# A fused scan and expert kernel on one core: the tile loop written out, its table read in place, and the silu turn and state sums moved between the two up-projections

## The reference, cut to what matters

```python
xn = layernorm(x)                                   # x: 2 x 2048 tokens of 256
# branch 1: a selective scan over tokens sorted by cluster
sort_idx = argsort(argmax(l2norm(xn) @ l2norm(means).T))
u = xn[sort_idx];  dts, Bm, Cm = split(u @ x_proj.T);  Cm += prompt[cluster]
delta = softplus(dts @ dt_w.T + dt_b);  A = -exp(A_logs)          # 16 states per channel
h = exp(delta * A) * h + delta * u * Bm             # one step per token, in order
y = sum_over_states(h * Cm) + Ds * u;  out1 = y[inverse of sort_idx]
# branch 2: two of eight experts for each token
out2[t] = sum over the 2 best e of p[t, e] * ((silu(xn @ w1[e]) * (xn @ w3[e])) @ w2[e])[t]
return x + out1 + out2
```

## Time and profile before

| | us |
|---|---|
| median of 3 runs | 819.19 (817.54 to 819.56) |
| the profiled execution | 817.38 |
| its span, first to last instruction | 815.3 |
| DVE busy in the span | 682.9 (84%) |
| PE busy | 663.9 (81%), matmuls |
| POOL busy | 597.3 (73%) |
| ACT busy | 431.0 (53%) |

### The profile page before, as it was taken

The page is one execution under the profiler, slowest core; times in us unless marked ns, Lnnn a source line. Parts: engine busy times, 40 slices in busy tenths (PEclk is TensorE's granted clock), DMA queues, the critical chain, the costliest instruction groups (busy, mean ns, idle before and its releaser), DMA issues. The chain is left out here.

```text
span 815.3 us, 15751 instructions
## 1 busy us (share of the span) xinstructions
PE 663.9 (81%) x4538; PEld 422.7 (52%) x4539; DVE 682.9 (84%) x882; ACT 431.0 (53%) x926; POOL 597.3 (73%) x372
## 2 busy tenths in 40 slices
PE   3734889788998798989998898999889798989870
PEld 2523745245655465556655565565556555655550
DVE  5769777579999999999999999999999999997110
ACT  1324656465655556656655575566557554653320
POOL 3728800038788898988989898888989898889532
PEclk9866955599999989999999998999999998999995
DMA  7972659979944754674575466547645654662322
GB/s 228 371 259 91 180 206 297 321 221 241 210 102 103 144 118 87 146 150 94 115 163 111 89 149 138 105 90 164 139 90 125 134 127 90 142 142 35 49 27 26
DMA packets 76845, 118.63 MB, mean 146 GB/s; under 512 B 22456, under 2 KB 56848, under 8 KB 74512
## 3 DMA queue, kind: packets, MB, share of 16 engines
q1 hardware_dynamic: 54656, 90.95, 41.2%
q0 software_dynamic: 19824, 27.16, 19.4%
q10 hardware_dynamic: 2336, 0.15, 0.2%
HBM read 82.87 MB, written 35.27 MB: 145 GB/s over the span
## 5 line engine op out<-in xcount | busy, mean ns | idle before, releaser
L534 POOL TENSOR_TENSOR ring<-ring,bc 128x1024 f32<-128x1024 f32 (+2 forms) x128 | 308.0, 2424 | 38.9 <-DVE state L1047 38.0
L1044 DVE TENSOR_TENSOR_SCAN ring<-ring,state,pb 128x512 f32<-128x512 f32 x256 | 313.8, 1267 | 4.6
L654 ACT ACTIVATE ring<-late,aneg 128x512 f32<-128x512 f32 x256 | 164.2, 721 | 12.0 <-DMA late<-dd_d 9.1
L1035 DVE TENSOR_TENSOR pb<-fb,bc 128x1024 f32<-128x1024 f32 x128 | 157.3, 1229 | 3.0
L1284 PE MATMUL py<-w2x,pool 128*128 x568 | 141.6, 395 | 0.5 <-ACT pool L726 0.3
L1267 PE MATMUL fa<-w,pool 128*128 x284 | 137.7, 608 | 3.9 <-issue 2.8
L506 POOL DMA_INDIRECT out_dram<-pool,meta x71 | 112.9, 1590 | 29.8 <-issue 15.7
L1267 PE MATMUL fb<-w,pool 128*128 x284 | 134.3, 596 | 0.0
L486 POOL DMA_INDIRECT pool<-xn_d,meta x71 | 71.3, 1004 | 81.3 <-DVE ids L1001 33.5
L1284 PEld LDWEIGHTS py<-w2x,pool 128*128 128x128 f32 x568 | 107.7, 200 | 13.6 <-issue 1.0
L1267 PEld LDWEIGHTS fb<-w,pool 128*128 128x128 f32 x284 | 54.5, 192 | 68.9 <-issue 68.9
(11 more groups left out here) (213 smaller groups left out, 752.8 us busy)
## 6 DMA issues: line engine op xcount, KB each, us to landing
late<-dd_d SPq DMA_DIRECT2D x256, 128.0 KB
bc<-bc_d SPq DMA_DIRECT2D x72, 256.0 KB
w<-in_L_ffn_w_dram SPq DMA_DIRECT2D x16, 512.0 KB, 8.6
ring<-in_L_attn_x_dram SPq DMA_DIRECT2D x8, 512.0 KB, 4.3
out_dram<-ring SPq DMA_DIRECT2D x8, 512.0 KB, 7.7
xn_d<-w2x SPq DMA_DIRECT2D x8, 512.0 KB, 8.6
dd_d<-pool SPq DMA_DIRECT2D x8, 512.0 KB
dd_d<-ring SPq DMA_DIRECT2D x8, 512.0 KB, 5.1
```

The costliest lines, as they stand in the source:

```text
L534: ins = po.tensor_tensor(r, r, c_rows, ALU.mult)
L654: ins = ac.activation(ring[:, g % RING, n, :], dd[:, g % 2, 0, :], ACT.Exp, scale=aneg[:, NH * g + n:NH * g + n + 1])
L1035: ve.tensor_tensor(pb[:, :].rearrange("p (n c) -> p n c", n=2), pd[:, :].rearrange("p (o c) -> p o c", o=1).to_broadcast([P, 2, CH]), b_ro ...
L1044: ve.tensor_tensor_scan(r, r, pb[:, CH * m:CH * m + CH], state[:, NH * g + n:NH * g + n + 1], ALU.mult, ALU.add).then_inc(S["scan_done"], 1)
```

## The change

- **Written out**: the loops are gone on all engines. 64 units and 71 tiles are straight code.
- **The table read in place**: POOL and ACT read `tab` themselves; `meta` and its 71 small transfers are gone. `ids` is read in place too, `ya` has two buffers, and `hand_over` with its two copies a chunk is gone. Gathered rows have 6 buffers (`XR`) and not 4, the scaled results 3 (`YE`) and not 2.
- **Another lag**: unit `u` now goes with tile `j = u - 1` and not `u + 1`. DVE starts unit 0 before any silu, and after unit 63 eight tiles are left (before: six). ACT starts with `put_du(0)`, `exps(0)`, and waits there for less.
- **PE's order in a tile**: `turn_h(j - 1)`, `turn_y` and `fold_states` now stand between the `w1` and the `w3` matmuls of tile `j`. In unit numbers, tile `v + 1` has `fold_states(v)` ahead of its `w3` matmuls.
- **Scan adds**: in steps 3 and 6 of a chunk (before 3 and 7). The last chunk's four go out together after the add of tile 65, not one by one between expert adds.
- **The last unit**: DVE multiplies its last two states by the C rows, POOL the first two. In the tiles after the scan, `turn_x` uses bank `pb`.

```diff
+UNITS = NCH * G
+REST = UNITS + 1
+SCAN_UNITS = {3: (0, 1), 6: (2, 3)}
+XR, XT, YE = 6, 4, 3
@@ sync @@
-            turn(0)
-            with sp.Fori(1, NCH) as c:
-                turn(c)
+            for u in range(UNITS):
+                c, g = u // G, u % G
+                if u >= 2:
+                    load_dd(u)
+                if c == 0 and g + EARLY < E:
+                    load_up(g + EARLY, w3, w3_in)
+                    load_down(g + EARLY)
...
@@ gpsimd @@
+            for u in range(UNITS):
+                c, g = u // G, u % G
+                j = u - 2
+                if j >= 0:
+                    gather(j + XR)
+                scans = SCAN_UNITS.get(g, ()) if c else ()
+                split = 1 if scans else NH // 2
+                po.wait_ge(S["h_ready"], u + 1)
+                done = multiply(u, slice(0, split))
+                for n in scans:
+                    add_scan(c - 1, n, landed_scan(c - 1, scans[0]) - 16)
+                if u < UNITS - 1:
+                    done = multiply(u, slice(split, NH))
+                elif split < NH // 2:
+                    done = multiply(u, slice(split, NH // 2))
+                done.then_inc(S["hc_done"], 1)
+                if j >= 0:
+                    add_expert(j)
+            for j in range(UNITS - 2, FT):
+                if j + XR < FT:
+                    gather(j + XR)
+                add_expert(j)
+                if j == LAST_SCANS:
+                    for n in range(TPC):
+                        add_scan(NCH - 1, n, landed_expert(j))
@@ scalar @@
+            def exps(u):
+                ac.wait_ge(dd_in[u % 2], 64 * (u // 2 + 1))
+                if u == 0:
+                    ac.wait_ge(S["pr_du"], KC * NCH)
+                elif u == 1:
+                    ac.wait_ge(S["bc_put1"], 32 * NCH // 2)
+                    ac.wait_ge(S["dd_put10"], 16 * NCH // 2)
+                elif u == 2:
+                    ac.wait_ge(S["dd_put11"], 16 * NCH // 2)
+                if u >= RING:
+                    ac.wait_ge(S["sum_done"], u - RING + 1)
...
+            put_du(0)
+            exps(0)
+            evac_xt(0)
+            exps(1)
+            for u in range(1, FT + 1):
+                j = u - 1
+                tanh(j)
+                if u < UNITS:
+                    put_du(u)
+                if j:
                     evac_ht(j - 1)
+                if 3 <= u < UNITS + 3:
+                    take_y(u - 3)
+                if 2 <= u < UNITS + 2:
+                    take_sum(u - 2)
                 if j + 1 < FT:
+                    evac_xt(j + 1)
+                if u + 1 < UNITS:
+                    exps(u + 1)
+                if j:
+                    evac_y(j - 1)
@@ vector @@
-            silu(0, 0)
...
+            for u in range(UNITS):
+                if u:
+                    silu(u - 1)
+                half_unit(u, 0)
+                half_unit(u, 1)
+                keep_states(u)
...
+            for j in range(UNITS - 1, FT):
+                silu(j)
@@ tensor @@
+            def sums_and_turns(u):
+
+                pe.wait_ge(S["ye_done"], u - 1)
+                if 3 <= u < UNITS + 3:
+                    turn_y(u - 3)
+                if u < UNITS + 2:
+                    fold_states(u - 2)
+            def up(j, e):
...
                     if w is w3:
                         expert_landed("w3_in", j, e)
-                        if not (isinstance(j, int) and j == 0):
+                        if j:
                             pe.wait_ge(S["silu_done"], j)
+                            turn_h(j - 1)
+                            sums_and_turns(j + 1)
```

More of the change, by code:

```diff
@@ L100, in program @@
         y1 = sb("y1", [P, P])
-        meta = sb("meta", [P, SPI, 2])
         tab = sb("tab", [P, FTP, 2])
@@ L243, in apart, with experts_by, scans_by, unit_of_expert @@
             eng.sem_inc(S["passed"], 1)
[L245 to L265, removed]
+        def experts_by(u):
+            return max(0, u - 1)
+        LAST_SCANS = UNITS + 1
+        def scans_by(u):
+            c, g = u // G, u % G
+            return 0 if c == 0 else (c - 1) * TPC + sum(len(SCAN_UNITS[k]) for k in SCAN_UNITS if k <= g)
+        def unit_of_expert(j):
+            return min(j + 2, UNITS - 1)
+        def landed_expert(j):
+            return 16 * (1 + j + 1 + scans_by(unit_of_expert(j)) + (TPC if j > LAST_SCANS else 0))
+        def landed_scan(c, n):
+            u = (c + 1) * G + next(k for k in SCAN_UNITS if n in SCAN_UNITS[k])
+            return 16 * (1 + experts_by(u - 1) + c * TPC + n + 1)
         @block.sync
@@ L509, in add_scan @@
-            def add_scan(turn, c, n, beside=0):
-                po.wait_ge(S["yb_done"], c + 1)
-                if not isinstance(c, int):
-                    apart(po)
-                po.wait_ge(S["added"], landed(turn - 1 - beside))
-                apart(po)
-                po.indirect_dma_start(out[:, :], bass.IndirectOffsetOnAxis(ap=idb[:, n:n + 1], axis=0), yb[:, n, :], None,
-                                      compute_op=ALU.add).then_inc(S["added"], 16)
-            po.wait_ge(S["acc_put"], 16 * NCH)
@@ L541, in _ @@
[L541 to L551 removed]
+            for j in range(2, XR):
+                gather(j)
@@ L664, in take_y, with put_du @@
-            def take_y(c, g, last=False):
-                u = unit_index(c, g)
+            def put_du(u):
+                if u:
+                    ac.wait_ge(S["dbu_done"], 2 * u)
+                else:
+                    ac.wait_ge(dd_in[0], 64)
+                    ac.wait_ge(S["pr_re"], KC * NCH)
+                ac.copy(pd[:, :], dd[:, u % 2, 1, :]).then_inc(S["du_put"], 1)
+            def take_y(u):
+                c, g = u // G, u % G
                 ac.wait_ge(S["ytr_done"], u + 1)
-                if not last:
+                if u + 1 < UNITS:
@@ L752, in turn @@
-            def turn(c):
-                exps(c, 0)
-                for s in range(SPI):
-                    j = SPI * c + 1 + s
-                    tanh(j, (s + 1) % 2)
-                    put_du(c, s)
-                    evac_ht(j - 1)
-                    take_units(c, s)
-                    ac.wait_ge(S["b_done"], j)
-                    evac_xt(j + 1, (s + 2) % 4)
-                    if s + 1 < SPI:
-                        exps(c, s + 1)
-                    if s == 2 and not isinstance(c, int):
-                        hand_over(c - 1)
-                    evac_y(j - 1, s % 2, s, expert_turn(c, s - 2) if s >= 2 else
-                           None if isinstance(c, int) else expert_turn(c - 1, SPI - 1) - (1 - s))
@@ L1333, in _ @@
[L1333 to L1340 removed]
+            turn_x(0)
+            e_down = expert_of(0)
+            up(0, e_down)
+            turn_x(1)
+            e_up = expert_of(1)
+            for j in range(1, FT):
+                u = j + 1
+                if j == G + 1:
+                    pe.wait_ge(S["w3_in"], 16 * E)
+                    pe.wait_ge(S["w2_in"], 16 * E)
+                up(j, e_up)
```

449 lines of the change are left out of this document (143 added, 306 removed).

## The result

The changed kernel takes 857.3 us in the median of 4 runs (855.1 to 859.22), the kernel before 819.23 beside it: a ratio of 1.0468, interval 1.0434 to 1.0502. It is slower by 38 us, where 853 was forecast. The profiled execution took 858.75, with a span of 857.0.

A forecast was written before the change was run, and what follows sets the result against it. DVE's step was taken to bound the main part. Unit 2 from 181.7 to 189.3, 61 steps of 8.89 and 53 us of stalls gave +37.7; less 2.8 at the end, 817.4 became 852, median 853; range 826 to 868.

The forecast's parts named there:

- The move of the sums: w3 behind fold_states: DVE stalls 2.05 (full clock) to 4.75 us, taken 3.8, in 14 scan-add steps: 53 us lost.
- rival (a): Scan-add steps: stalls come but PE's clock stays up, 14 x 2.05 = 29 us, so 828 us; chance 0.18 with mixtures.
- Rival (b): Steps 3 and 6: scan adds don't hold the bank up, so the change gains: 799 us; chance 0.11.
- Rival (c): The late unit spreads to the next step, 1 us more each, full 4.75 stalls: 880 us; chance 0.08 beyond 866.
- The loops: Main part: without loops and their waits every DVE step takes 8.89 us, not 9.03: 8.5 us gained.
- The start: Before unit 2: it starts at 181.7, not 188.6, about 7 us gained; bounds 4 and 8.4.
- The end: Behind unit 63: the last add starts 56.7 us after it, not 59.5, so 2.8 us gained.
- The sum: Whole kernel: +37.7 us up to unit 63's end, less 2.8 at the end: 852 profiled, 853 median.

The follow-up runs named there:

- experiment 1: The changed kernel with turn_h, turn_y and fold_states behind the w3 matmuls again, all else kept: 811.55 us, ratio 0.9929 to the kernel before.
- experiment 4: The kernel before, its loops and lag kept, with only PE's new order (turn_h, turn_y, fold_states between w1 and w3): 875.39 us, ratio 1.070.
- Experiment 2: The changed kernel with four more matmuls on PE ahead of fold_states in the 14 scan-add steps: 831.73 us, ratio 1.016 to the kernel before.
- experiment 8: The changed kernel with one scan add in each of steps 1, 3, 5 and 7, not two in steps 3 and 6: 832.48 us, ratio 1.028.
- experiment 7: Experiment 6 with the last four scan adds behind the add of tile 64, not of tile 65: 796.56 us, ratio 0.9871 to the kernel before.
- Experiment 6: Experiment 1 with the change's order for tiles behind the scan, and unit 2's load ahead of the weight loads: 801.2 us, ratio 0.9894.
- experiment 9: Experiment 7 with four more 128x256 matmuls on PE ahead of fold_states in the 14 scan-add steps: 802.77 us, ratio 0.9791, on another chip.
- experiment 3: The changed kernel with the scan adds of steps 3 and 6 issued behind POOL's whole multiply and hc_done: 903.81 us, ratio 1.104.

## Why the prediction was right, and where it was not

**The move of the sums: right in place, kind and size.** 14 stalls were put at 3.8 us, 53 in all. There are 14, from 288.66 to 791.83, between 2.48 and 4.78 long, 53.3 in all. The links measured in the step shown: multiply 8.6 (forecast 8.6), PE's pause 4.90 (4.4), fold and `w3` 1.94 and 3.78 (1.94 and 3.7), bank ready at 14.3 (14.4). Experiments 1 and 4 show that the order is the cause, from either kernel: 44 us off, 57 us on. Experiment 2 shows the step's mechanism: with the clock kept up the stall is the 2.08 that stood as the lower bound. That is rival (a)'s price, which so needs matmuls in the pause that the change didn't have. Rival (b) fell with the 8.6: the adds do hold the bank up, and experiment 8 shows that even one of them takes all the slack. Rival (c) did not come: steps behind a stall are 8.89.

The Trainium skill's page "TensorE: Matmul & The Clock Gate", section "Part 1: The HAM clock gate", says that the clock has two levels. The trace agrees: the fold takes 1.08 or 1.94 and `w3` 1.98 or 3.78 at one level, with values between where the clock changed within, and the granted clock is 0.50 in the stretches that were read. Behind all 14 pauses of 4.9 to 5.4 the clock was down for most of the fold or all of it (1.67 to 1.94), and in 12 of them it came back within `w3` (2.5 to 3.1). The first stalls have the full 4.7 us; the later ones, 3.5 to 4.1, are the mixture that the 3.8 left room for. I chose 3.8 between 2.05 and 4.75 by the nearest pause and not by a rule, so its closeness is partly luck.

**One of the 14 fell elsewhere.** 13 lie between units and lengthen their steps by 50.4 us. The last, behind unit 62, is one step later than its unit and so falls behind unit 63: the first row of the tail, at 791.83.

```profile
791.83 0.69 DVE L989 SCALAR_TENSOR_TENSOR pool<-pool,fb 128x512 f32<-128x512 f32 x1 [2.48 <-PE fb L1201]
```

**The loops: right for a step, too much for the sum of them.** From unit 2's start, 62 units end at 787.5. 183.69 + 7.6 + 61 x 8.89 is 733.6; with 50.4 for the stalls and 3.1 for two more waits (below) it is 787.1. What is left over is 0.4, of which 0.28 is a `memset` of the states between the two sequences of tokens, so a step without a wait is 8.89 as forecast. The rule of the Trainium skill's page "Runtime: NRT & Kernel Launch", section "Instruction fetch mechanics", that straight code is streamed ahead, agrees with this: an ordinary step of the 64 written out has no idle on DVE, while before, the first step of the loop's body began with some 0.4 us in which DVE waited for nothing that the profile shows. One such row of the kernel before:

```profile
385.60 0.69 DVE L1069 SCALAR_TENSOR_TENSOR pool<-pool,fa 128x512 f32<-128x512 f32 x1 [0.44 <-issue]
```

But some 2.2 of the 8.5 us were waits of single steps for ACT and PE (0.74 and three of 0.47), not the loop's. Such waits came back once the stalls were gone: in experiment 1 units 4 to 62 took 8.97 each, and in experiment 7 8.96, where 8.89 was forecast and 9.03 stood before. So not all of the 8.5 us was to be had.

**The start: 2.0 us too early.** Unit 1 was right to 1.3 (170.70, forecast 172). Unit 2 stood at 183.69 and not 181.7: its load, behind four weight loads, let ACT start `exps(2)` at 179.28, where 177 was taken. Experiment 6 shows the cause: with the load ahead of the weights the idle is gone. The gain was 5 us and not 7. The forecast's upper bound of 8.4 was itself a slip, for it took the moment at which `tanh(1)` is ready for the start of unit 2; one step behind unit 1's 172 is 180.9, a gain of 7.7.

**Two waits in chunk 0 that I had not seen: 3.1 us.** Both were released by PE. The larger, on the timeline of the changed kernel:

```profile
209.27 1.60 POOL L449 DMA_INDIRECT out_dram<-pool,tab  x1 [3.42 <-DMA out_dram<-pool,tab]
...
216.91 1.62 PE L1126 MATMUL py<-ring,fold 128*32 128x128 f32 x32 [1.02 <-POOL ring L462]
...
218.46 3.08 PE L1201 MATMUL fb<-w,pool 128*128 x4
...
221.66 0.69 DVE L989 SCALAR_TENSOR_TENSOR pool<-pool,fb 128x512 f32<-128x512 f32 x1 [2.19 <-PE fb L1201]
```

POOL stands 3.42 us for the add before to land, in the stretch in which the weights still come in. It is the same chain, POOL late, fold late, `w3` late, set off by a slow add and not by scan adds. That the weight loads slowed the add is likely and was not tested by itself.

**The end: no gain of 2.8 but a loss of 0.8.** The last add stands 60.3 behind unit 63, forecast 56.7, before 59.5. The term that failed is where tile 65's add starts: 27.6 behind the unit, not 23.4. From the trace of the changed kernel:

```profile
793.95 1.88 PE L1201 MATMUL fa<-w,pool 128*128 x4
...
815.12 1.56 POOL L449 DMA_INDIRECT out_dram<-pool,tab  x1 [4.69 <-ACT pool L683]
...
825.23 1.55 POOL L456 DMA_INDIRECT out_dram<-late,ids  x1 [0.31 <-issue]
...
847.81 1.55 POOL L449 DMA_INDIRECT out_dram<-pool,tab  x1 [2.93 <-DMA out_dram<-pool,tab]
```

The add waits for ACT's scaling, so for PE, and PE begins `w1` of tile 64 (793.95) 6.5 behind unit 63, not 1.6. The forecast let PE start there as in an ordinary step, though by its own count unit 62's stall falls just there: `w3` of tile 63 stands behind the late fold. From `w1` to the add it is 21.2, forecast 21.8, and from there the sum was right: 32.7 to the last add, forecast 33.3; the four scan adds go out 1.86 apart.

**The sum.** The profiled execution is 858.75 where 852 was forecast. 2.0 at the start, 3.1 in chunk 0, 2.8 less in the scan (13 stalls and not 14), 0.4 left over, 3.6 at the end, and 0.1 in what follows the last add and what lies around the span: 6.4, against a difference of 6.75 and of 6.4 before the sum was rounded. The 2.8 and the 3.6 are one slip: the fourteenth stall was counted in the scan and left out of the end.

## What to carry to other kernels

Ahead of an instruction that fills a single buffer for the bounding engine, put nothing that waits on a third engine, unless the slack (here 1.7 us) covers that engine's worst step, not its common one. Cost a stall on TensorE at half clock if its pause grows, and see whether spare matmuls in the pause are cheaper than the clock. An order that is bad where another engine bounds can be the good one in the tail: choose it by stage, and when you move a transfer, count the wait for its landing in the queue that it comes to stand in.

## What the runs showed of the hardware that was not expected

- **More matmuls, less time.** Four extra matmuls in each of 14 steps took the changed kernel from 857 to 832 us. The granted clock, as a mean over the kernel, went from 0.896 to 0.932. Behind `w3` the ratio with them was 0.979 against 0.987, on two chips, so that there the gain is not shown.
- **The clock does not fall behind each pause of a length.** Behind a pause of 2.63 us the fold took 1.08 in experiment 8, and behind one of 2.65 in the same execution 1.94. Behind one of 3.19 in experiment 7 it took 1.08 too but the down-projection behind it 3.35; behind one of 2.40 in experiment 9 the fold took 1.93. The rows of experiment 8 and then of 9:

```profile
712.28 1.94 PE L1126 MATMUL py<-ring,fold 128*32 128x128 f32 x32 [2.65 <-POOL ring L462]
```

```profile
595.24 1.93 PE L1128 MATMUL py<-ring,fold 128*32 128x128 f32 x32 [2.40 <-POOL ring L464]
```

What else decides stays open.
- **The landing of adds.** In the quiet tail of the changed kernel POOL waited 2.9 to 3.0 us for an add before it to land, and no longer (3.01) behind four scan adds sent out together. Behind the pairs within the scan of experiment 3 it was 3.9 to 6.1, mostly about 4. What makes the difference was not tested.
- **The chip matters more than some edits.** The kernel before took 809.4 us on one chip and 818.3 to 819.4 on the two others. In the profiled executions of the experiments' kernels, 5 to 7 us of such a difference lay ahead of the scan.
